# Delta-rule decoder, one core: the running inverse X summed in PSUM and copied out by ScalarE, and three vector-engine operations of step 4 in another place

## The chip, the core and the metric

The kernel runs on one core of a Trainium2 chip. A core has TensorE (PE, with its weight loads shown apart as PEld), VectorE (DVE), ScalarE (ACT), GpSimd (POOL) and SyncE (SP, which only issues transfers here). Each takes its own instructions strictly in order and waits on semaphores that others raise. The metric is device time in microseconds (us) of one execution; less is better.

## The reference

The whole is a decoder block over x (4 batches, 512 tokens, 128 features): a spiking gated delta-rule attention with a feed-forward part, then cross attention, then a three-layer feed-forward net. The change lies in the first part alone, whose recurrence is, per token, batch and head (8 heads, key size 64, value size 128):

```python
mem = DECAY * mem + sdt
hard = (mem > THR).astype(x.dtype)
spike = sur + jax.lax.stop_gradient(hard - sur)
mem = mem - spike * THR
alpha = jax.nn.sigmoid(abt + alpha_spike * spike)
beta = jax.nn.sigmoid(bbt[..., None] + jnp.sum(spike * beta_spike, axis=-1, keepdims=True))
...
s = s * alpha[..., None]
u = jnp.einsum('bhd,bhdv->bhv', kt, s)
s = s - beta[..., None] * jnp.einsum('bhd,bhv->bhdv', kt, u)
s = s + beta[..., None] * jnp.einsum('bhd,bhv->bhdv', kt, vt)
out = jnp.einsum('bhdv,bhd->bhv', s, qt)
```

The kernel doesn't run it token by token. It takes chunks of 64 tokens, so that the corrections inside a chunk become a triangular system of 64 by 64 for each head. The inverse of that system is what the change is about.

## The kernel before

**Rounds.** There are 8 chunks times 4 batches = 32 rounds, one chunk of one batch with all 8 heads in each. `rounds(body)` calls the same `body` on every engine for i = -3 to 32, and one call works on several rounds at once: `prev` (i-1) is written out, `cur` (i) reads and updates the state, `nxt` (i+1) has its triangular matrix inverted, `aft` (i+2) has the matrix entries formed level by level, and `aft2` (i+3) gets its first level. `gate` and `gate_old` (chunk gates i+7 and i+6, up to i = 24 and 25) compute alpha and beta for later chunks, and `scan` (up to i = 20) runs 32 single operations of the spike recurrence, `charge` (L199) and `fire` (L203) by turns, each of which needs the one before it. They are strewn between the other operations of the vector engine by `spike(scan, h)`.

**Steps.** A body has five steps, l = 1 to 5. In step l, TensorE runs for `nxt` `make_z` (L970: Z = E·X for this level), `make_x` (L980, for l up to 4) and `make_xt` (L994), and then for `aft` `level` (L935: the matrix entries of level l). Before, what `make_x` leaves in PSUM is added to X in SBUF by the vector engine (`add_x`, L642), what `make_xt` leaves is added to the transposed inverse XT by `add_xt` (L647), and ScalarE copies Z out of PSUM between them (`copy_z`, L1285). After `level`, the vector engine runs `prefix` (L608), `suffix` (L620) and `keep` (L637) for `aft`; `level` of step l+1 waits for the three of step l.

**What stands around them.** On TensorE in step 3: `values(cur)` (L1003) between Z and X, `correct(cur)` (L1011) and `turn_out(prev)` (L1089: transposes of the normalised output) after `level`; in step 4 `solve(cur)` (L1020), `spike_sums` and `spike_counts` of the gate; in step 5 `read_state` (L1034), `write_state` (L1082). On ScalarE: four `square` (L1330) in steps 1 and 2, `normalise(prev)` (L1338, four activations, after which `turn_out` may run) and `keep_res` (L1318) in step 3, `keep_u` (L1322), `start_xt` (L1295, L1297) and `keep_out` (L1357, whose end `read_state` of step 5 waits for) in step 4, `soft_alpha` (L1345) and `fade` (L1312) in step 5, `copy_start` (L1302: the first X of `aft`) last. On the vector engine: `scale_key` (L590) and `scale_query` (L594) of `aft2`, and `alpha` (L674) of the gate in step 5. `level` of step 5 waits for `alpha`, since both use the same PSUM banks.

All orders are written out by hand in the four `body` functions; no scheduler changes them.

Of the kernel before, what the change touches and what calls it, by code (L numbers as in the profile page):

```python
# [25 lines left out]
def decoder_kernel(nc, x, ctx_in, vec_in, wq, wk, w_spike, wv, w_out, w_au, w_ad, w_beta, w_u1, w_u2,  # L26
# [6 lines left out]
    C = 64  # L33
# [11 lines left out]
    with ctx:  # L45
# [216 lines left out]
        psZX = paired(6)  # L262
        psZX_half = psZX[:, :, 0:W]
        psXT = psG[:, B * C:B * C + HP * W].rearrange("p (a n) -> p a n", a=HP)
# [55 lines left out]

        x0_out = psZX[:, :, 0:C]

# [59 lines left out]
        def by_chunk(t):  # L382
            return t.rearrange("p (b t) -> p b t", b=B)

        GATES = NC * HP
# [16 lines left out]
        with nc.Block() as block:  # L402
# [142 lines left out]
            def _(ve):  # L545
# [50 lines left out]
                def prefix(n, l):  # L596
                    ve.wait_ge(lvl_mm, n.it * LEVELS + l + 1)
                    ve.wait_ge(kq_ok, n.it * NKQ + l + 1)
# [31 lines left out]
                def keep(n, l):  # L630
# [6 lines left out]
                    ve.copy_predicated(kept, late, level_out(l).rearrange("p a x j t -> p x a j t")).then_inc(e_ok, 1)  # L637

                def add_x(n, l):
                    ve.wait_ge(x_mm, n.it * NX + l)  # L640
                    at_ = first_half(X, l)
                    ve.tensor_tensor(at_, at_, packed(psZX_half, l), ALU.add).then_inc(x_ok, 1)  # L642

# [52 lines left out]
                def body(prev, cur, nxt, aft, aft2, gate, gate_old, scan, ramp):  # L696
                    for l in range(1, NINV + 1):
                        h = 6 * (l - 1)
                        if ramp == 0 and l != 3:
                            four_scales(1 + l // 4, (l % 4) // 2 if l < 4 else l - 4)  # L700
                        if ramp == 1 and l < 3:
                            four_scales(3, l - 1)
                        spike(scan, h)
                        if nxt and l < NINV:
                            add_x(nxt, l)
                        if l == 5 and gate:
                            alpha(gate)
# [11 lines left out]
                        spike(scan, h + 4)  # L719
                        if aft:  # L720
                            keep(aft, l)
                        spike(scan, h + 5)
# [97 lines left out]
            def _(pe):  # L820
# [88 lines left out]
                def level(n, l, gate=None, gate_old=None):  # L909
# [4 lines left out]
                    if n.it == 0 and l == 0:  # L914
# [4 lines left out]
                        pe.wait_ge(qk_ok, NQK)  # L919
                    pe.wait_ge(kq_ok, n.it * NKQ + l + 1)  # L920
                    if l == 0:
# [17 lines left out]
                def turn_start(n):  # L939
                    if n.it == 0:  # L940
                        pe.wait_ge(sd_ok, NSD)
                        pe.wait_ge(qk_ok, NQ_ALL)
                    pe.wait_ge(x_init, n.it + 1)
                    pe.wait_ge(x_ok, n.it * NX)
                    for head in by_time:
                        (rows, a), (to, q) = at_xt(*head), at_x(*head)
                        last = pe.matmul(x0_out[to, q], XT[rows, n.two, a], eye[rows], start=True, stop=True)
                    last.then_inc(x0_mm, 1)
# [11 lines left out]
                def make_z(n, l):  # L960
# [7 lines left out]
                    for head in by_time:  # L968
                        (rows, a), (_, q), (to, z) = at_level(*head), at_x(*head), at_z(*head)
                        last = pe.matmul(packed(psZX_half, l)[to, z], EA[rows, n.three, l, a], first_half(X, l)[rows, q],  # L970
                                         start=True, stop=True)
                    last.then_inc(z_mm, 1)

                def make_x(n, l):
# [227 lines left out]
            def _(ac):  # L1202
# [80 lines left out]
                def copy_z(n, l):  # L1283
                    ac.wait_ge(z_mm, n.it * NINV + l)
                    ac.copy(first_half(Z[:, l - 1], l), packed(psZX_half, l)).then_inc(z_ok, 1)  # L1285

# [13 lines left out]
                def copy_start(n):  # L1300
                    ac.wait_ge(x0_mm, n.it + 1)
                    ac.copy(X, x0_out).then_inc(x0_ok, 1)  # L1302

# [57 lines left out]
                def body(prev, cur, nxt, aft, aft2, gate, gate_old, scan, ramp):  # L1361
                    for l in range(1, NINV + 1):
# [5 lines left out]
                        if l == 1 and gate_old:  # L1368
                            soft_beta(gate_old)
                        if l == 1 and prev:  # L1370
                            square(prev, 0)
                            square(prev, 1)
                        if l == 2 and nxt:
                            keep_ks(nxt)
                        if l == 2 and prev:
                            square(prev, 2)
                            square(prev, 3)
# [4 lines left out]
                        if l == 4 and cur:  # L1382
                            keep_u(cur)
                        if l == 4 and aft:
                            start_xt(aft)
                        if l == 4 and prev:
                            keep_out(prev)
                        if l == 5 and gate:
# [906 lines left out]
```

## Time and profile before

| | |
|---|---|
| time, median of 3 runs | 1092.09 us (1091.55 to 1096.4) |
| the profiled execution | 1096.75 us, span 1095.0 us |
| share of the span busy | PE 89%, PEld 59%, DVE 64%, ACT 44%, POOL 19% |

"Busy" is the time in which an engine had at least one instruction in flight; waiting for semaphores isn't in it. The span has three parts: a prologue to about 154 us, the rounds to about 704 us, and cross attention with the last net from there. A row of the timeline gives start, length, engine, line, what is written from what, how many instructions, and in brackets how long the engine sat idle before and who ended that. The line numbers are those of the kernel before; in the changed kernel the same functions stand some 5 to 10 lines lower.

### The profile page before, as it was taken

What the parts mean: (1) busy time and instruction counts of PE and PEld (TensorE: products, weight loads), DVE (VectorE), ACT (ScalarE), POOL (GpSimd) and SP (SyncE); (2) the same over time, 40 slices, a digit from 0 to 9 for tenths busy, and PEclk for the clock granted to TensorE, in tenths of its full rate; (3) what the DMA queues carried; (4) which work ended last, traced back from release to release, by engine and by line L of the source; (5) the groups of instructions that cost most, each with busy time, mean ns of one, the idle gap of its engine ahead of it and who ended that gap; (6) DMA issues with size and microseconds to landing.
All of it is one profiled execution on the core that took longest, in us unless ns stands there. A gap on an engine that the chain in (4) does not pass through costs nothing. (4 is left out here: it accounts for less than half of the span.)

```text
span 1095.0 us, 40049 instructions
## 1 busy us (share of the span) xinstructions
PE 972.4 (89%) x16722; PEld 648.9 (59%) x16722; DVE 698.6 (64%) x2514; ACT 482.7 (44%) x1378; POOL 208.7 (19%) x394
## 2 busy tenths in 40 slices
PE   7878768999998999999999888679999999999996
PEld 2333247777777777777777777446446546546542
DVE  2887886989889888898877765145424524714710
ACT  7667412555555555545555555313323423423311
POOL 7100201122122121221221220221210310310300
PEclk8999956999999999999999999889999999999999
DMA  3000000000000000000000000211000000100100
GB/s 97 0 1 1 1 1 3 4 4 4 4 4 4 4 4 4 4 4 4 4 5 11 22 4 4 96 37 27 7 1 21 24 1 15 27 1 3 31 1 10
DMA packets 18652, 13.83 MB, mean 13 GB/s; under 512 B 2491, under 2 KB 17259, under 8 KB 18475
## 3 DMA queue, kind: packets, MB, share of 16 engines
q1 hardware_dynamic: 18475, 11.28, 3.5%
q8 instruction: 135, 2.21, 0.9%
q14 instruction: 42, 0.34, 0.1%
HBM read 7.70 MB, written 1.05 MB: 8 GB/s over the span
## 5 line engine op out<-in xcount | busy, mean ns | idle before, releaser
L935 PE MATMUL banks<-work 64*64 64x64 f32 x3072 | 97.9, 234 | 24.9 <-DVE gates L674 12.9
L994 PE MATMUL banks<-work 64*64 64x32 f32 x2560 | 107.6, 224 | 5.8 <-ACT work L1351 5.0
L1285 ACT COPY work<-banks 128x128 f32<-128x128 f32 x160 | 42.8, 268 | 157.8 <-PE banks L970 157.7
L199 DVE SCALAR_TENSOR_TENSOR gates<-mom,gates 128x16 f32<-128x16 f32 x512 | 101.1, 197 | 9.5 <-ACT gates L1258 4.5
L203 DVE SCALAR_TENSOR_TENSOR mom<-gates 128x16 f32<-128x16 f32 x512 | 102.9, 201 | 5.0
L994 PEld LDWEIGHTS banks<-work 64*64 64x64 f32 x2560 | 92.5, 139 | 18.1 <-issue 10.0
L637 DVE COPY_PREDICATED gates<-work,banks 128x256 f32<-128x256 uint32 x192 | 101.9, 531 | 1.1
L935 PEld LDWEIGHTS banks<-work 64*64 64x64 f32 x3072 | 73.0, 139 | 43.2 <-issue 20.5
L531 POOL TENSOR_TENSOR mom<-mom 128x4 f32<-128x4 f32 x32 | 7.2, 223 | 384.4 <-ACT work L1330 384.4
L608 DVE TENSOR_TENSOR work<-work 128x256 f32<-128x256 f32 x160 | 67.8, 424 | 19.3 <-PE banks L935 18.7
L647 DVE TENSOR_TENSOR work<-work,banks 128x128 f32<-128x128 f32 x160 | 45.6, 285 | 48.4 <-PE banks L994 45.4
L970 PE MATMUL banks<-work,gates 64*64 64x32 f32 x2560 | 72.7, 221 | 2.1 <-issue 1.5
L970 PEld LDWEIGHTS banks<-work,gates 64*64 64x64 f32 x2560 | 59.4, 137 | 10.2 <-issue 7.1
L980 PEld LDWEIGHTS banks<-work 64*64 64x64 f32 x2048 | 42.8, 137 | 37.1 <-issue 22.0
L1698 PE MATMUL banks<-qT,gates 128*128 128x512 f32 x128 | 59.2, 598 | 3.4 <-ACT kT L1983 2.6
L980 PE MATMUL banks<-work 64*64 64x32 f32 x2048 | 57.0, 228 | 5.8 <-ACT work L1285 2.6
L642 DVE TENSOR_TENSOR work<-work,banks 128x128 f32<-128x128 f32 x128 | 36.6, 286 | 32.3 <-PE banks L980 31.8
L1312 ACT ACTIVATE work<-work 128x128 f32<-128x128 f32 x128 | 40.9, 390 | 23.9 <-PE banks L1034 23.9
L1629 POOL TENSOR_TENSOR work<-work,half 128x4 f32<-128x4 f32 x16 | 16.1, 1009 | 185.2 <-DVE work L2099 185.2
L620 DVE TENSOR_TENSOR work<-work 128x128 f32<-128x128 f32 x160 | 46.8, 293 | 0.0
L1633 POOL TENSOR_TENSOR work<-work,gates 128x1232 f32<-128x1232 f32 x12 | 27.0, 2248 | 102.5 <-DVE gates L2205 102.5
L1034 PE MATMUL banks<-work 64*64 64x128 f32 x512 | 41.9, 278 | 5.1 <-ACT kT L1357 5.0
(263 smaller groups left out, 2140.8 us busy)
## 6 DMA issues: line engine op xcount, KB each, us to landing
work<-gates SPq DMA_DIRECT2D x28, 38.5 KB
qT<-in_x_dram SPq DMA_DIRECT2D x4, 256.0 KB, 3.8
work<-in_x_dram SPq DMA_DIRECT2D x4, 256.0 KB, 2.9
out_dram<-work SPq DMA_DIRECT2D x4, 256.0 KB, 2.3
gates<-in_w_ff_dram SPq DMA_DIRECT2D x3, 256.0 KB, 3.2
wv_sb<-in_wv_dram SPq DMA_DIRECT2D x1, 512.0 KB, 4.6
work<-in_w_out_dram SPq DMA_DIRECT2D x1, 512.0 KB, 4.0
gates<-in_x_Wq_dram SPq DMA_DIRECT2D x1, 512.0 KB, 5.0
```

The lines of the kernel that those rows point to most:

```text
L199: ve.scalar_tensor_tensor(mem[:, :, t], neg_mem, -0.9, mem[:, :, t], ALU.mult, ALU.add).then_inc(charged, 1)
L203: ve.scalar_tensor_tensor(neg_mem, mem[:, :, t], 1.0, mem[:, :, t], ALU.is_gt, ALU.subtract)\
L608: ve.tensor_tensor(second, second, by, ALU.mult).then_inc(kq_ok, 1)
L620: ve.tensor_tensor(first, first, by, ALU.mult).then_inc(ks_ok, 1)
L637: ve.copy_predicated(kept, late, level_out(l).rearrange("p a x j t -> p x a j t")).then_inc(e_ok, 1)
L647: ve.tensor_tensor(at_, at_, packed(psXT, l), ALU.add).then_inc(xt_ok, 1)
L935: last = pe.matmul(level_out(l)[to, a], KS[rows, n.two, hp], late[rows, hp], start=True, stop=True)
L970: last = pe.matmul(packed(psZX_half, l)[to, z], EA[rows, n.three, l, a], first_half(X, l)[rows, q], start=True, stop=True)
L980: last = pe.matmul(packed(psZX_half, l)[to, q], XT[rows, n.two, a], first_half(Z[:, l - 1], l)[rows, z], start=True, stop=True)
L994: last = pe.matmul(packed(psXT, l)[rows, a], Z[rows, l - 1, z], second_half(XT[:, n.two], l)[rows, a], start=True, stop=True)
L1285: ac.copy(first_half(Z[:, l - 1], l), packed(psZX_half, l)).then_inc(z_ok, 1)
L1698: last = pe.matmul(ps[:, :], w1_sb[:, a, f * P:(f + 1) * P], H1(b)[:, a, :], start=a == 0, stop=a == F2 - 1)
```

## The change

1. X lives in PSUM. Each head has 256 columns in the pair of banks; X takes the first 64, and each level's Z now has 32 columns of its own behind them. `turn_start` opens the sum and `make_x` adds to it by accumulation. `make_x` now writes the columns of X that belong to it, blocks of 2, 4, 8 and 16 columns with gaps as long, where before it wrote 32 adjacent ones.
2. `add_x` (vector engine) is gone. ScalarE has `copy_x` in its place, after `make_x` of the same step: PSUM to SBUF, half of X's columns.
3. ScalarE's order: a `square` on either side of `copy_x` in steps 1 and 2; `copy_x` ahead of `normalise` in step 3; `keep_u`, `copy_x`, `keep_out`, `start_xt` in step 4.
4. Vector engine, step 4: `scale_query` and two scan operations stand ahead of `add_xt`, and nothing of them is left behind `keep`. `prefixed` adapts the count that `prefix` and `level` wait for.

```diff
-                        if nxt and l < NINV:
-                            add_x(nxt, l)
                         if l == 5 and gate:
                             alpha(gate)
                         spike(scan, h + 1)
+                        if l == 4 and aft2:
+                            scale_query(aft2)
+                        if l == 4:
+                            spike(scan, h + 2)
+                            spike(scan, h + 3)
                         if nxt:
                             add_xt(nxt, l)
                         if l == 4 and gate:
                             drive(gate)
-                        spike(scan, h + 2)
+                        spike(scan, h + (4 if l == 4 else 2))
                         if aft:
                             prefix(aft, l)
-                        spike(scan, h + 3)
+                        spike(scan, h + (5 if l == 4 else 3))
...
-                        if l == 4 and aft2:
-                            scale_query(aft2)
...
+        def prefixed(n, l):
+            early = l == LEVELS - 1 and n.it + 1 < ROUNDS
+            return n.it * NKQ + l + 1 + early
...
-                        last = pe.matmul(packed(psZX_half, l)[to, q], XT[rows, n.two, a],
-                                         first_half(Z[:, l - 1], l)[rows, z], start=True, stop=True)
+                        last = pe.matmul(first_half(x_out, l)[to, q], XT[rows, n.two, a],
+                                         first_half(Z[:, l - 1], l)[rows, z], start=False, stop=l == NX,
+                                         skip_group_check=True)
...
+                def copy_x(n, l):
+                    ac.wait_ge(x_mm, n.it * NX + l)
+                    ac.copy(first_half(X, l), first_half(x_out, l)).then_inc(x_ok, 1)
```

ScalarE, one body in the middle of the rounds. Before (L1285 is `copy_z`):

```order
L1285 COPY work<-banks 128x64x2
L1351 ACTIVATE work<-banks,vec 128x256
L1330 ACTIVATE work,mom<-banks 128x128 x2
L1285 COPY work<-banks 128x32x4
L1306 COPY work<-banks 128x256
L1330 ACTIVATE work,mom<-banks 128x128 x2
L1285 COPY work<-banks 128x16x8
L1338 ACTIVATE work<-banks,mom 128x128 x4
L1318 COPY work<-banks 128x512
L1285 COPY work<-banks 128x8x16
L1322 COPY work<-banks 128x512
L1295 COPY work<-gates 128x128
```

The same place now, steps 3 and 4 (L1291 is `copy_z`, L1295 `copy_x`, L1348 `normalise`, L1328 `keep_res`, L1332 `keep_u`, L1367 `keep_out`, L1305 and L1307 `start_xt`):

```order
L1291 COPY work<-banks 128x16x8
L1295 COPY work<-banks 128x16x8
L1348 ACTIVATE work<-banks,mom 128x128 x4
L1328 COPY work<-banks 128x512
L1291 COPY work<-banks 128x8x16
L1332 COPY work<-banks 128x512
L1295 COPY work<-banks 128x8x16
L1367 COPY qT<-banks 128x2x2x64
L1367 COPY kT<-banks 128x2x2x64
L1305 COPY work<-gates 128x128
L1307 COPY work<-gates 64x128 x2
```

In step 3 one copy came between `copy_z` and `normalise`; in step 4 `keep_out` and `start_xt` have changed places.

Vector engine, end of step 4 and start of step 5. Before, from `suffix` (L620) to `alpha` (L674):

```order
L620 TENSOR_TENSOR work<-work 128x8x16
L199 SCALAR_TENSOR_TENSOR gates<-mom,gates 128x16
L637 COPY_PREDICATED gates<-work,banks 128x2x8x16
L203 SCALAR_TENSOR_TENSOR mom<-gates 128x16
L594 TENSOR_TENSOR work<-qT,gates 128x256
L199 SCALAR_TENSOR_TENSOR gates<-mom,gates 128x16
L674 SCALAR_TENSOR_TENSOR gates<-banks,work 128x4x64
```

The same place now (L626 is `suffix`, L643 `keep`, L675 `alpha`):

```order
L626 TENSOR_TENSOR work<-work 128x8x16
L643 COPY_PREDICATED gates<-work,banks 128x2x8x16
L199 SCALAR_TENSOR_TENSOR gates<-mom,gates 128x16
L675 SCALAR_TENSOR_TENSOR gates<-banks,work 128x4x64
```

Between `suffix` and `alpha` two scan operations and `scale_query` have gone; they stand ahead of `add_xt` of step 4. TensorE's order is the same in both kernels.

## Rows read from the trace of the kernel before

**Rows 1.** Busy time by stretch; columns as its own header says.
```profile
core 0: us, PE busy (x) PEld busy (x) DVE busy (x) ACT busy (x) POOL busy (x), PEclk, DMA share, GB/s
154.40:194.95 40.55, 36.06 (x830) 29.50 (x832) 28.62 (x132) 10.07 (x31) 5.12 (x14) 0.63 0.01 3
194.95:532.18 337.23, 310.91 (x9366) 248.91 (x9363) 293.14 (x1361) 179.76 (x640) 75.43 (x180) 1.00 0.02 4
532.18:597.36 65.18, 61.17 (x1882) 49.64 (x1880) 47.65 (x151) 35.61 (x129) 14.71 (x36) 1.00 0.02 4
```

**Rows 2.** `copy_start` (L1302), once a body: 195 to 532 us, then 532 to 597.
```profile
L1302 ACT COPY work<-banks x20: 347/372/373, 194.9 to 515.4; 128x256 f32<-128x256 f32 x20
...
L1302 ACT COPY work<-banks x4: 349/350/374, 532.2 to 581.3; 128x256 f32<-128x256 f32 x4
```

**Rows 3.** TensorE's waits, 195 to 532 us: us in total, times, longest.
```profile
PE banks L935 <- DVE gates L674: 9.9, 20, 0.6
PE banks L930 <- DVE gates L637: 4.9, 17, 0.3
PE banks L994 <- ACT work L1351: 4.0, 20, 0.2
PE banks L935 <- DVE gates L637: 3.0, 15, 0.2
```

**Rows 4.** Timeline, end of step 4 and start of step 5 of one body.
```profile
411.58 0.51 ACT L1345 ACTIVATE work<-gates,vec 128x256 f32<-128x256 f32 x1
411.73 0.18 DVE L199 SCALAR_TENSOR_TENSOR gates<-mom,gates 128x16 f32<-128x16 f32 x1
411.82 0.43 DVE L637 COPY_PREDICATED gates<-work,banks 128x256 f32<-128x256 uint32 x1
412.14 0.43 PEld L994 LDWEIGHTS banks<-work 64*64 64x64 f32 x11
412.16 0.19 DVE L203 SCALAR_TENSOR_TENSOR mom<-gates 128x16 f32<-128x16 f32 x1
412.26 0.42 DVE L594 TENSOR_TENSOR work<-qT,gates 128x256 f32<-128x256 f32 x1
412.59 0.19 DVE L199 SCALAR_TENSOR_TENSOR gates<-mom,gates 128x16 f32<-128x16 f32 x1
412.69 0.42 DVE L674 SCALAR_TENSOR_TENSOR gates<-banks,work 128x256 f32<-128x256 f32 x1
413.16 0.15 PEld L935 LDWEIGHTS banks<-work 64*64 64x64 f32 x4 [0.59 <-DVE gates L674]
```

**Rows 5.** Timeline, step 3 of the same body.
```profile
404.53 0.27 ACT L1285 COPY work<-banks 128x128 f32<-128x128 f32 x1 [1.20 <-PE banks L970]
404.78 1.14 ACT L1338 ACTIVATE work<-banks,mom 128x128 f32<-128x128 f32 x4
405.42 0.43 PE L980 MATMUL banks<-work 64*64 64x32 f32 x16
405.92 0.29 DVE L642 TENSOR_TENSOR work<-work,banks 128x128 f32<-128x128 f32 x1
406.94 0.66 PE L1089 MATMUL banks<-ident,work 128*128 128x128 f32 x4
407.09 0.58 ACT L1318 COPY work<-banks 128x512 f32<-128x512 f32 x1 [1.17 <-PE banks L1011]
407.78 0.65 PE L1020 MATMUL banks<-work 64*64 64x128 f32 x16
```

**Rows 6.** TensorE's wait for `keep_out`, 597 to 704 us.
```profile
PE banks L1034 <- ACT kT L1357: 5.0, 6, 1.3
```

**Rows 7.** Timeline, step 4 of a body without gates.
```profile
639.56 0.30 ACT L1295 COPY work<-gates 128x128 f32<-128x128 f32 x1
640.38 0.36 ACT L1357 COPY qT<-banks 128x256 f32<-128x256 f32 x1
641.16 0.55 PE L1034 MATMUL banks<-work 64*64 64x128 f32 x6 [0.44 <-ACT kT L1357]
```

**Rows 8.** Groups by shape, 195 to 530 us: busy us, mean ns, idle before.
```profile
L642 DVE TENSOR_TENSOR work<-work,banks 128x128 f32<-128x128 f32 x80 | 22.6, 282 | 9.0 <-PE banks L980 8.7
L1285 ACT COPY work<-banks 128x128 f32<-128x128 f32 x100 | 26.8, 268 | 97.2 <-PE banks L970 97.2
L980 PE MATMUL banks<-work 64*64 64x32 f32 x1280 | 34.9, 224 | 2.2
L1011 PE MATMUL banks<-work 64*64 64x128 f32 x320 | 13.6, 272 | 0.1
```

More of the change, by code:

```diff
@@ L319, in level_out, with z_out @@
             return level_at.rearrange("p a (x j t) -> p a x j t", x=2, t=1 << l)
-        x0_out = psZX[:, :, 0:C]
+        x_out = psZX[:, :, 0:C]
+        def z_out(l):
+            return psZX[:, :, C + W * (l - 1):C + W * l].rearrange("p a (j t) -> p a j t", t=1 << l)
         def counts(g):
@@ L712, in body @@
                             drive(gate)
-                        spike(scan, h + 2)
+                        spike(scan, h + (4 if l == 4 else 2))
                         if aft:
                             prefix(aft, l)
-                        spike(scan, h + 3)
+                        spike(scan, h + (5 if l == 4 else 3))
                         if aft:
                             suffix(aft, l)
-                        spike(scan, h + 4)
+                        if l != 4:
+                            spike(scan, h + 4)
                         if aft:
                             keep(aft, l)
-                        spike(scan, h + 5)
+                        if l != 4:
+                            spike(scan, h + 5)
                         if l == 1 and gate:
@@ L919, in level @@
                         pe.wait_ge(qk_ok, NQK)
-                    pe.wait_ge(kq_ok, n.it * NKQ + l + 1)
+                    pe.wait_ge(kq_ok, prefixed(n, l))
                     if l == 0:
@@ L946, in turn_start @@
                         (rows, a), (to, q) = at_xt(*head), at_x(*head)
-                        last = pe.matmul(x0_out[to, q], XT[rows, n.two, a], eye[rows], start=True, stop=True)
+                        last = pe.matmul(x_out[to, q], XT[rows, n.two, a], eye[rows], start=head[0] == 0, stop=False,
+                                         skip_group_check=True)
                     last.then_inc(x0_mm, 1)
@@ L969, in make_z @@
                         (rows, a), (_, q), (to, z) = at_level(*head), at_x(*head), at_z(*head)
-                        last = pe.matmul(packed(psZX_half, l)[to, z], EA[rows, n.three, l, a], first_half(X, l)[rows, q],
-                                         start=True, stop=True)
+                        last = pe.matmul(z_out(l)[to, z], EA[rows, n.three, l, a], first_half(X, l)[rows, q],
+                                         start=False, stop=True, skip_group_check=True)
                     last.then_inc(z_mm, 1)
@@ L1284, in copy_z @@
                     ac.wait_ge(z_mm, n.it * NINV + l)
-                    ac.copy(first_half(Z[:, l - 1], l), packed(psZX_half, l)).then_inc(z_ok, 1)
+                    ac.copy(first_half(Z[:, l - 1], l), z_out(l)).then_inc(z_ok, 1)
+                def copy_x(n, l):
+                    ac.wait_ge(x_mm, n.it * NX + l)
+                    ac.copy(first_half(X, l), first_half(x_out, l)).then_inc(x_ok, 1)
                 def start_xt(n):
@@ L1301, in copy_start @@
                     ac.wait_ge(x0_mm, n.it + 1)
-                    ac.copy(X, x0_out).then_inc(x0_ok, 1)
+                    ac.copy(X, x_out).then_inc(x0_ok, 1)
                 def keep_ks(n):
@@ L1369, in body @@
                             soft_beta(gate_old)
-                        if l == 1 and prev:
-                            square(prev, 0)
-                            square(prev, 1)
                         if l == 2 and nxt:
                             keep_ks(nxt)
-                        if l == 2 and prev:
-                            square(prev, 2)
-                            square(prev, 3)
+                        if l < 3 and prev:
+                            square(prev, 2 * l - 2)
+                        if l == 4 and cur:
+                            keep_u(cur)
+                        if nxt and l < NINV:
+                            copy_x(nxt, l)
+                        if l < 3 and prev:
+                            square(prev, 2 * l - 1)
                         if l == 3 and prev:
@@ L1381, in body @@
                             keep_res(cur)
-                        if l == 4 and cur:
-                            keep_u(cur)
+                        if l == 4 and prev:
+                            keep_out(prev)
                         if l == 4 and aft:
                             start_xt(aft)
-                        if l == 4 and prev:
-                            keep_out(prev)
                         if l == 5 and gate:
```

8 lines of the change are left out of this document (2 added, 6 removed).

## The prediction

> **What bounds the kernel now.** I read first the busy time by stretch, to see which engine fills the rounds. Over 195 to 532 us, with TensorE's granted clock at 1.00 (its 2.4 GHz level), PE is busy 310.91 of 337.23 us and the vector engine 293.14 [rows 1]. Both are near full, so the share alone doesn't say which one binds. The count of `copy_start` gives the length of a body: 20 bodies in 337.23 us are 16.86 us each, and 4 bodies in 65.18 us are 16.3 us each [rows 1, 2]. The second stretch is the test: the scan has ended there, and the vector engine does 47.65 / 4 = 11.9 us a body where it did 293.14 / 20 = 14.7 us. It lost 2.8 us of work, and the body became only 0.56 us shorter. So the vector engine's load is not what binds; TensorE's order of work is, with whatever it waits for. I then read TensorE's waits: in 20 bodies it waits 9.9 us for `alpha` (20 times), 4.9 us for the last `keep` before `level` 0, 4.0 us for `soft_beta`, 3.0 us for other `keep`s [rows 3]. Together 21.8 us, 1.1 us a body. It never waits for `add_x`. An edit gains what it takes from this list, and loses what it adds to it.
>
> **Taking `add_x` off the vector engine.** It removes 4 operations of 282 ns a body [rows 8], 1.13 us. No row of TensorE's waits names L642, and the vector engine itself waits for PE there (8.7 us in 80) [rows 8]. In step 3 of the body I followed, `add_x` ran at 405.92, right behind `make_x`, while TensorE went on with `make_xt` [rows 5]. The waits of 3.0 us on `keep` are at the ends of chains that begin at `level`, behind `add_x`. I take 0 for this edit, with 3.0 us as the most that it can give; below nothing it can't go, since it only removes work from an in-order engine.
>
> **`scale_query` and two scan operations moved.** Here the gain lies. At the end of step 4, `keep` starts at 411.82, `scale_query` at 412.26, `alpha` at 412.69, and TensorE's `level` of step 5 starts at 413.16 after 0.59 us of waiting [rows 4]. Gone from ahead of `alpha` are: the slot of `scale_query`, 412.59 - 412.26 = 0.33; of one scan operation behind `keep`, 412.26 - 412.16 = 0.10; of one ahead of it, 411.82 - 411.73 = 0.09. Sum 0.52 us, so `alpha` starts at 412.17. What else could hold it then: `soft_alpha` ends at 411.58 + 0.51 = 412.09, just earlier. TensorE's own work ahead of `level` ends at 412.14 + 0.43 = 412.57, and `alpha` would let it go at 413.16 - 0.52 = 412.64. So nearly the whole wait goes: 9.9 us less 20 times some 0.02 = **9.5 us**. The moved operations land in the time in which the vector engine waits for `make_xt` of step 4, so they cost nothing; were that cover gone, they would cost 0.52 us a body again, and the gain would be 0. Behind `level` the chain to the next wait (`level`, `prefix`, `suffix`, `keep`, `level` 0) moves as a whole, so its 4.9 us stay. Bounds: 0 to 9.9.
>
> **`copy_x` on ScalarE, steps 1, 2 and 4.** I take 0.27 us for it, the time of `copy_z`, of the same size and source [rows 8]. In these steps ScalarE is free soon enough and X is needed only by the next step's `make_z`, which TensorE reaches after `make_xt` and `level`. ScalarE's busy time would go from 180 to about 202 of 337 us, so it has the room.
>
> **`copy_x` in step 3: a new wait.** ScalarE is in order, and `copy_x` now stands ahead of `normalise` and `keep_res`. Before, `normalise` started at 404.78, right behind `copy_z`. `make_x` starts only at 405.42, since `values` stands between; its result was taken by the vector engine at 405.92. So `copy_x` can run from 405.92 to 406.19, and `normalise`, 1.14 us long, until about 407.32. TensorE's `turn_out`, which waits for it, started at 406.94 [rows 5]. With 0.05 us for the signal it now starts at 407.37: 0.43 us late. TensorE is in order, so `make_z` of step 4, `solve` and all the rest stand behind it. `keep_res`, behind `normalise` too, runs from 407.32 to 407.90, and `solve`, moved from 407.78 to 408.21, doesn't feel it. Does a later wait soak this up? The chain to `alpha` starts at `level` of step 4, behind `turn_out`, and moves along; nor do I find another. This holds for each i from 1 to 30 (both `prev` and `nxt` there): 30 times 0.43 = **12.9 us lost**. Bounds: nothing, if something in the body soaks it up, and 16 us if the strided copy takes as long as the copy of 256 columns, 0.37 us [rows 2].
>
> **ScalarE's step 4.** In the last bodies, which have no gates, TensorE waits for `keep_out`: 5.0 us in six waits, the longest 1.3 [rows 6]. `keep_out` now stands ahead of `start_xt`. In the body that I followed `start_xt` began at 639.56 and `keep_out` at 640.38 [rows 7]: 0.82 us, of which `copy_x` takes about 0.26, so it comes 0.56 us sooner. A wait of 0.44 goes whole; a wait of 1.3 keeps 0.7. With two waits below 0.56 and four above I get about 3.2 us; `start_xt`, later by 0.9 us, then presses on `copy_z` of step 5, so I take **3.0 us**. Bounds: 0 and 3.4.
>
> **The accumulating matmuls.** They take as many passes as before. No row of before shows an accumulating write with gaps; `correct` accumulates without gaps at 272 ns for 128 columns, `make_x` overwrites at 224 ns for 32 [rows 8]. As a lower end I take 0, as an upper end the length of a group with four times the columns: `solve` 0.65 against `make_x` 0.43 [rows 5], 0.22 us, four times in 30 bodies = 26 us. I take 0: `correct` and `solve`, of one size, the one accumulating and the other not, follow one another in step 3 and 4 without a difference that I could price.
>
> **The sum.** 1096.75 - 9.5 - 3.0 + 12.9 = 1097.2 us for the profiled execution. That one lies 4.7 us above the median of the runs, 1092.09; carried over, **1092.5 us**. Two true effects, each about 1%, cancel. A measurement of this kernel can tell some 0.5%, 5.5 us, from no change.
>
> **Rivals.** (A) The vector engine binds after all: it is busy 87% of the rounds, and each operation of it costs time. Then 20 bodies save 1.13 us, 22.6 us, and the time is about 1070. Against it stand the bodies without the scan. (B) The new wait in step 3 is hidden, because ScalarE gets `copy_x` done sooner or TensorE reaches `turn_out` later than in the body that I followed: 1092.1 - 12.5 = 1079.6. For it: an intermediate value would do much the same, and one body is a small sample. Against it: `make_x` to `turn_out` is 1.5 us here, and copy, `normalise` and signals need 2. (C) Slower: the wait in step 3 comes as worked out, but `alpha` doesn't come sooner, because it waits for `soft_alpha`, which ends only 0.08 us ahead of the new place [rows 4]. It decides from the point at which ScalarE reaches step 5 over 0.5 us late, by `start_xt` behind `keep_out`. Then 1092.1 + 12.9 - 3.0 = 1102. (D) The writes with gaps make `make_x` slow: up to 1092.5 + 26 = 1118.
>
> On (D) the Trainium skill speaks: the page "PSUM — Partial Sum Buffer", section Specifications, says that PSUM has cachelines of 8 bytes and that any access pattern that isn't contiguous slows matmuls significantly. "Advanced Engine Details and Errata", section PSUM Cachelines, adds that every two consecutive elements should be contiguous. By the first, all four `make_x` are hit; by the second none, since the smallest block here is two elements. No run here shows either.
>
> **How the numbers follow.** The forecast, all terms as summed: 0.52. (A) 0.07, (B) 0.15, (C) 0.18, (D) 0.08. The forecast's own range, from the bounds of its terms near the values taken, is 1087 to 1098. A range that holds the time 8 times in 10 must take in (B) and (C): 1079 to 1103, which leaves out (A) and (D), 0.15. Faster by over 0.5%: (A), (B) and 0.02 of the forecast's edge, 0.24. Slower: (C), (D), 0.26. Within: 0.50.
>
> **What the profile will show.** TensorE's waits: L935 for `alpha` falls from 9.9 us to under 1; a new row for `turn_out` waiting for `normalise`, about 0.4 us in each body; L1034's wait for `keep_out` falls from 5.0 to about 2. ScalarE waits for `make_x` in step 3. The vector engine's busy time in the rounds falls by 36 us, and it idles more. I am wrong if `turn_out` shows no wait, if `alpha` still holds `level`, or if `make_x` got longer.

## The result

Over 20 runs of each kernel the median went from 1095.3 to 1088.4 us. The ratio of the runs, after to before, is **0.9934**, with a 95% interval of 0.9913 to 0.9955: 0.66% faster, some 7 us, where I had forecast no change. The forecast stood on a base of three runs (1092.1 us), which lies 3 us below the median of these 20, so ratios and differences are compared here and not bare times. The profiled execution of after took 1094.59 us (span 1092.9) and lies high among its runs, so I compare stretches and not spans.

The same 20 bodies that took 337.23 us before [rows 1] take 330.02 us now (columns of the first line: us, then busy time by engine, granted clock):

```profile
core 0: us, PE busy (x) PEld busy (x) DVE busy (x) ACT busy (x) POOL busy (x), PEclk, DMA share, GB/s
194.84:524.86 330.02, 307.61 (x9368) 246.82 (x9366) 287.25 (x1281) 191.55 (x722) 74.66 (x180) 1.00 0.02 4
654.00:671.00 17.00, 16.04 (x464) 13.63 (x464) 7.84 (x24) 9.07 (x37) 1.21 (x2) 0.80 0.01 3
```

That is 7.2 us, the whole of the gain. The last line shows why the profiled execution isn't as fast as its rounds: near the end of the rounds TensorE, busy 16.04 of 17.00 us, was granted a mean clock of 0.80, part of the time the lower level of 1.2 GHz. In the same stretch of before it was busy 14.85 us and was granted 1.00. I draw nothing from it.

TensorE's waits over those bodies, answering to [rows 3] (us in total, times, longest):

```profile
PE banks L1000 <- ACT work L1361: 4.0, 20, 0.2
PE banks L934 <- DVE gates L643: 3.8, 13, 0.3
PE banks L939 <- DVE gates L643: 3.6, 18, 0.2
PE banks L1095 <- ACT work L1348: 1.8, 7, 0.3
PE banks L951 <- issue: 1.6, 2, 0.8
PE banks L1079 <- issue: 1.2, 3, 0.5
PE banks L1017 <- issue: 0.8, 2, 0.5
PE banks L975 <- issue: 0.7, 1, 0.7
```

The wait for `alpha`, 9.9 us before, is gone. `turn_out` (L1095) now waits for `normalise` (L1348), as forecast, but by this view for 1.8 us where I had worked out 0.43 us in each body. And rows with "issue" as the releaser have come up, 4.3 us in these four where before had 1.1: in them the view names nothing that TensorE waited for. What they are is worked out near the end.

The view of waits counts only what stands out as a gap between matmuls whose ends are modelled, so it isn't a full account. A better one is the time from the start of one group of matmuls to the start of the next, taken from the timeline and averaged over the same 20 bodies of each kernel (in before those from 196 to 533 us). Only few places move from before to after; the rest agree within 0.05 us. For use below, all kernels stand in it:

```
from -> to (us, mean)      before after  e1    e2    e3    e4    e5    e6    e7    e8
make_xt 2 -> level 2        0.78  0.83  0.84  0.81  0.83  0.83  0.82  0.83  0.63  0.63
level 2 -> make_z 3         0.45  0.28  0.48  0.27  0.30  0.28  0.27  0.45  0.31  0.30
make_xt 3 -> level 3        0.53  0.53  0.49  0.52  0.53  0.52  0.50  0.87  0.93  0.40
correct -> turn_out         0.62  0.86  0.61  0.82  0.58  1.00  0.61  0.60  0.57  0.64
make_xt 5 -> level 5        1.15  0.62  0.63  1.15  0.61  0.62  0.63  0.63  0.63  0.64
turn_start -> level 0       1.57  1.64  1.62  1.57  1.69  1.64  1.63  1.68  1.49  1.51
whole body                 16.86 16.50 16.51 16.82 16.47 16.73 16.36 16.95 16.57 16.12
```

The line of whole bodies is good to some 0.1 us: e3 and e5 differ only in the order of ScalarE's step 4, every other line agrees within 0.06 us, and the bodies still differ by 0.11.

Before to after: -0.53 at level 5 (`alpha`), +0.24 at `turn_out`, -0.17 between level 2 and `make_z` of step 3, and about +0.1 spread over several places. Sum -0.36 us a body, 7.2 us in 20.

Step 3 of one body of after, which answers to [rows 5] (L1291 is `copy_z`, L985 `make_x`, L1295 `copy_x`, L1348 `normalise`, L1095 `turn_out`, L1026 `solve`):

```profile
399.63 0.27 ACT L1291 COPY work<-banks 128x128 f32<-128x128 f32 x1 [0.87 <-PE banks L975]
400.51 0.43 PE L985 MATMUL banks<-work 64*64 64x32 f32 x16
401.02 0.27 ACT L1295 COPY work<-banks 128x128 f32<-128x128 f32 x1 [1.12 <-PE banks L985]
401.18 1.15 ACT L1348 ACTIVATE work<-banks,mom 128x128 f32<-128x128 f32 x4
402.38 0.65 PE L1095 MATMUL banks<-ident,work 128*128 128x128 f32 x4 [0.28 <-ACT work L1348]
403.22 0.65 PE L1026 MATMUL banks<-work 64*64 64x128 f32 x16
```

From the start of `make_x` to `turn_out` it is 1.87 us. `make_x`, now accumulating and writing with gaps, takes 0.43 us for its 16, exactly as before [rows 5]; the median of one matmul of it is 219 ns in both traces. And `normalise` starts 0.16 us after `copy_x` starts, not 0.27.

### The profile page after: what moved, and what is told of

It is laid out like the page before. It is cut to its first block and busy times, and to the rows that moved or that the text cites. A ratio compares the mean times of both kernels' runs of the same rounds, so it can differ in the third digit from the quotient of the medians.

```text
span 1092.9 us, 40049 instructions
## 1 busy us (share of the span) xinstructions
PE 978.3 (90%) x16722; PEld 652.6 (60%) x16722; DVE 682.3 (62%) x2386; ACT 503.7 (46%) x1506; POOL 208.7 (19%) x394
## 3 DMA queue, kind: packets, MB, share of 16 engines
q8 instruction: 135, 2.21, 0.8%
## 5 line engine op out<-in xcount | busy, mean ns | idle before, releaser
L1291 ACT COPY work<-banks 128x128 f32<-128x128 f32 x160 | 42.8, 268 | 134.1 <-PE banks L975 134.0
L199 DVE SCALAR_TENSOR_TENSOR gates<-mom,gates 128x16 f32<-128x16 f32 x512 | 98.5, 192 | 9.5 <-ACT gates L1264 4.5
L1000 PEld LDWEIGHTS banks<-work 64*64 64x64 f32 x2560 | 93.5, 140 | 18.2 <-issue 10.2
L643 DVE COPY_PREDICATED gates<-work,banks 128x256 f32<-128x256 uint32 x192 | 101.8, 530 | 1.1
L648 DVE TENSOR_TENSOR work<-work,banks 128x128 f32<-128x128 f32 x160 | 45.8, 286 | 88.5 <-PE banks L1000 86.6
L939 PEld LDWEIGHTS banks<-work 64*64 64x64 f32 x3072 | 74.3, 140 | 31.4 <-issue 20.7
L985 PEld LDWEIGHTS banks<-work 64*64 64x64 f32 x2048 | 43.7, 139 | 38.1 <-issue 22.6
L985 PE MATMUL banks<-work 64*64 64x32 f32 x2048 | 57.8, 230 | 6.0 <-ACT work L1291 2.7
L1295 ACT COPY work<-banks 128x128 f32<-128x128 f32 x128 | 34.5, 269 | 43.1 <-PE banks L985 42.8
L626 DVE TENSOR_TENSOR work<-work 128x128 f32<-128x128 f32 x160 | 46.3, 289 | 0.0
```

The lines of the kernel that those rows point to most:

```text
L199: ve.scalar_tensor_tensor(mem[:, :, t], neg_mem, -0.9, mem[:, :, t], ALU.mult, ALU.add).then_inc(charged, 1)
L626: ve.tensor_tensor(first, first, by, ALU.mult).then_inc(ks_ok, 1)
L648: ve.tensor_tensor(at_, at_, packed(psXT, l), ALU.add).then_inc(xt_ok, 1)
L939: last = pe.matmul(level_out(l)[to, a], KS[rows, n.two, hp], late[rows, hp], start=True, stop=True)
L985: last = pe.matmul(first_half(x_out, l)[to, q], XT[rows, n.two, a], first_half(Z[:, l - 1], l)[rows, z], start=False, stop=l == NX, skip_g ...
L1000: last = pe.matmul(packed(psXT, l)[rows, a], Z[rows, l - 1, z], second_half(XT[:, n.two], l)[rows, a], start=True, stop=True)
```

## The experiments

Each was timed against the kernel before on the same chip: e1 to e4 on one, e5 to e7 on another, e8 on a third.

### e1: the vector engine's moves alone

The kernel before with `scale_query` and two scan operations ahead of `add_xt` in step 4; X stays in SBUF.

```diff
+                        if l == 4 and aft2:
+                            scale_query(aft2)
+                        if l == 4:
+                            spike(scan, h + 2)
+                            spike(scan, h + 3)
                         if nxt:
                             add_xt(nxt, l)
...
-                        if l == 4 and aft2:
-                            scale_query(aft2)
```

> The kernel before with the vector engine's moves of step 4 alone (scale_query and two scan operations ahead of add_xt); X stays in SBUF, add_x stays on the vector engine. Theory of waits (W): the wait of level 5 for alpha, 9.9 us in 20 bodies, goes whole, nothing else moves: ratio to before 0.991, about -10 us; the row of L935 waiting for alpha falls under 1 us. Rival (V), the gain of the changed kernel comes from the vector engine's lighter load: this one has the same load, so 1.000.

Measured: 0.9939 (0.9918 to 0.996). The vector engine has the same work as before (busy 296.3 us in the 20 bodies, before 293.1) and nearly the whole gain is there, so the lighter load isn't its cause. TensorE's wait for `alpha` is gone from the list. The gain is 6.7 us and not 10, which lies just outside what the interval allows (4.4 to 9.0 us). Some came back as issue rows:

```profile
PE banks L1082 <- issue: 1.4, 3, 0.8
PE banks L956 <- issue: 0.8, 1, 0.8
PE banks L944 <- issue: 0.7, 2, 0.4
PE banks L979 <- issue: 0.7, 2, 0.4
```

### e2: X in PSUM alone

The changed kernel with the vector engine's step 4 in its old order.

```diff
-                        if l == 4 and aft2:
-                            scale_query(aft2)
-                        if l == 4:
-                            spike(scan, h + 2)
-                            spike(scan, h + 3)
                         if nxt:
                             add_xt(nxt, l)
...
+                        if l == 4 and aft2:
+                            scale_query(aft2)
```

> The changed kernel with the vector engine's step 4 in its old order: X in PSUM, copy_x and ScalarE's new order stay. W: the wait for alpha is back (about 10 us); turn_out waits for normalise, about +0.24 us in each of 30 bodies (+7 us); make_z of step 3 no longer waits for add_x of step 2 (-0.17 us a body, -3 to -5 us); keep_out comes sooner in the last bodies (-3 us). Sum -1 to +1 us, ratio 0.999 to 1.001. V: most of the gain stays, 0.994.

Measured: 1.0015 (0.9993 to 1.0037), which agrees with the 0.999 to 1.001 expected. This half of the change takes four operations a body from the vector engine (busy 283.5 us in the 20 bodies, before 293.1) and gains nothing: the wait for `alpha` is back, and `turn_out` waits.

```profile
PE banks L934 <- DVE gates L675: 9.8, 20, 0.5
PE banks L929 <- DVE gates L643: 5.5, 19, 0.3
PE banks L1090 <- ACT work L1343: 2.2, 8, 0.3
```

It also isolates the term that I had missed. With `copy_x` on ScalarE, `make_z` of step 3 starts 0.27 us after level 2 (column e2 of the table); in both kernels with `add_x`, before and e1, it is 0.45 and 0.48. The rows of before show why, once one looks at the right place (L642 is `add_x`, L970 `make_z`):

```profile
403.56 0.35 PEld L935 LDWEIGHTS banks<-work 64*64 64x64 f32 x16 [0.28 <-issue]
403.62 0.28 DVE L642 TENSOR_TENSOR work<-work,banks 128x128 f32<-128x128 f32 x1
404.01 0.35 PEld L970 LDWEIGHTS banks<-work,gates 64*64 64x64 f32 x16
```

Here the weight loads of level 2 end at 403.91, `add_x` ends at 403.90, and `make_z` begins at 404.01. `add_x` of step 2 stands behind `keep` of step 1, which is also what level 2 waits for, so both come out together, and the next `make_z` needs `add_x`. The start of that `make_z` lies 0.15 us behind the end of `add_x` in all 20 bodies of before, in 19 of 20 of e1 and in 19 of 20 of e6, so it is `add_x` that lets it go, and 0.45 us is not TensorE's own pace. In after, `copy_x` was done long before:

```profile
398.22 0.27 ACT L1295 COPY work<-banks 128x128 f32<-128x128 f32 x1
398.79 0.42 PEld L939 LDWEIGHTS banks<-work 64*64 64x64 f32 x16 [0.29 <-issue]
399.10 0.35 PEld L975 LDWEIGHTS banks<-work,gates 64*64 64x64 f32 x16
```

### e3: `copy_x` of step 3 behind `normalise`

```diff
-                        if nxt and l < NINV:
+                        if nxt and l < NINV and l != 3:
                             copy_x(nxt, l)
...
                         if l == 3 and prev:
                             normalise(prev)
+                        if l == 3 and nxt:
+                            copy_x(nxt, l)
```

> The changed kernel with copy_x of step 3 behind normalise instead of ahead of it. W: turn_out doesn't wait any more; that gives back 0.24 us in each of 30 bodies, about 7 us: ratio to before 0.987. By the step of my prediction (0.43 us a body, 12.9 us) it would be 0.982. If the wait is hidden anyway: 0.993 as the changed kernel.

Measured: 0.9901 (0.9873 to 0.9928). In the trace the wait of `turn_out` is gone (0.86 to 0.58 in the table). The time is 0.0033 better than that of the change, under half of what 0.28 us a body would give, and the two intervals overlap. The bodies became only 0.03 us shorter in this profile; waits with issue as releaser took the difference:

```profile
PE banks L1079 <- issue: 2.0, 3, 0.7
PE banks L951 <- issue: 1.8, 2, 1.1
PE banks L939 <- issue: 1.7, 5, 0.6
PE banks L975 <- issue: 1.0, 2, 0.6
```

### e4: a second copy ahead of `normalise`

```diff
                     ac.wait_ge(x_mm, n.it * NX + l)
-                    ac.copy(first_half(X, l), first_half(x_out, l)).then_inc(x_ok, 1)
+                    if l == 3:
+                        ac.copy(X[:, 0:2], x_out[:, 0:2])
+                        ac.copy(X[:, 2:4], x_out[:, 2:4]).then_inc(x_ok, 1)
+                    else:
+                        ac.copy(first_half(X, l), first_half(x_out, l)).then_inc(x_ok, 1)
```

> The changed kernel with copy_x of step 3 done as two copies of 128x128 (whole X of two heads of four each), so that normalise starts one ScalarE slot, about 0.17 us, later. W: the time from the start of make_x to turn_out has a floor, 1.86 us in the changed kernel; it becomes 2.03, and only bodies that were above it already hide the rest: 24 of 30 bodies lose up to 0.17 us, about +4 us over the changed kernel, ratio to before 0.997. If the wait is soaked up elsewhere: 0.993.

Measured: 0.9956 (0.9938 to 0.9974), 0.0022 slower than the change, in the direction and about half of the size expected; the two intervals overlap. In the table `turn_out` comes 0.15 us later (0.86 to 1.00), close to the slot of 0.17. And the time from the start of `make_x` to `turn_out`, whose floor was expected to go from 1.86 to 2.03 us, is 2.03 or 2.04 in 17 of the 20 bodies. So the delay follows the length of what stands ahead of `normalise`. In time this shows best between e4 and e3, which differ only in what stands there: 0.9956 and 0.9901, 0.0055 apart with intervals that don't meet, some 6 us where the table's 0.43 us in 30 bodies makes 13.

```profile
PE banks L1095 <- ACT work L1352: 6.4, 18, 0.5
```

### e5: `start_xt` ahead of `keep_out` again

```diff
+                        if l == 4 and aft:
+                            start_xt(aft)
                         if l == 4 and prev:
                             keep_out(prev)
-                        if l == 4 and aft:
-                            start_xt(aft)
```

> e3_copy_behind with ScalarE's step 4 in its old order, start_xt ahead of keep_out, copy_x where it is in the change. If the term for keep_out (3.0 us, six waits of the last bodies) was right, this is 3 us slower than e3_copy_behind: ratio to before 0.993 against 0.990. If those waits only moved elsewhere: 0.990. In the trace L1040 waits for keep_out again, near 5 us in six waits.

Measured: 0.99 (0.9867 to 0.9932), the same as e3. The waits are back in the trace:

```profile
PE banks L1040 <- ACT kT L1367: 5.2, 6, 1.3
```

From `make_z` of step 5 to `read_state` the last four bodies that have both sum to 4.86 us in before, 1.95 in after, 2.55 in e3 and 5.14 here, so the new order takes 2.6 to 2.9 us off these waits. But the time doesn't show it. Both intervals are some 3 us wide to either side, so a term of 3 us can neither be confirmed nor ruled out here. It stays open.

### e6: `add_x` of step 2 sooner

e1 with the gate's `spikes` operation behind `add_x`.

```diff
                         if nxt and l < NINV:
                             add_x(nxt, l)
+                        if l == 2 and gate:
+                            spikes(gate)
...
-                        if l == 1 and gate:
-                            spikes(gate)
```

> e1_move_only (X in SBUF, add_x on the vector engine) with the gate's spikes operation, 0.29 us, moved from the end of step 1 to behind add_x of step 2. Theory: make_z of step 3 starts 0.45 us after level of step 2 where 0.25 is its pace, because it waits for add_x of step 2; this edit starts add_x 0.2 us sooner, so that start comes at 0.27 or less, about 0.17 us a body in 20 bodies, 3.4 us: ratio to before 0.991 against 0.994 of e1_move_only. Rival, that the 0.45 us are TensorE's own pace: 0.994 and an unchanged 0.45.

Measured: 0.9976 (0.9953 to 0.9998), slower than e1. A miss. `add_x` of step 2 started with level 2 as before (0.01 us behind its start, 0.03 in e1) and the 0.45 us stayed, so the edit didn't test what it was meant to test: two scan operations that need one another now stand side by side, the second starts 0.26 us after the first where 0.1 is usual.

```profile
268.20 0.22 DVE L203 SCALAR_TENSOR_TENSOR mom<-gates 128x16 f32<-128x16 f32 x1
268.46 0.19 DVE L199 SCALAR_TENSOR_TENSOR gates<-mom,gates 128x16 f32<-128x16 f32 x1
268.56 0.28 DVE L646 TENSOR_TENSOR work<-work,banks 128x128 f32<-128x128 f32 x1
```

What it lost is a new wait: level 3 (L944) waited 5.9 us in 14 for `beta` (L685), the last operation of step 2.

### e7: the scan out of the chains

e3, with no scan operations between `prefix`, `suffix` and `keep` in steps 1 and 5. They stand behind `keep`, in step 1 two of them behind `spikes`; the last two of step 5 stand between the updates of the state that follow it.

```diff
-                        spike(scan, h + (5 if l == 4 else 3))
+                        tight = l == 1 or l == 5
+                        if not tight:
+                            spike(scan, h + (5 if l == 4 else 3))
                         if aft:
                             suffix(aft, l)
-                        if l != 4:
+                        if l != 4 and not tight:
                             spike(scan, h + 4)
                         if aft:
                             keep(aft, l)
                         if l != 4:
-                            spike(scan, h + 5)
+                            spike(scan, h + (3 if tight else 5))
                         if l == 1 and gate:
                             spikes(gate)
+                        if l == 1:
+                            spike(scan, h + 4)
+                            spike(scan, h + 5)
...
```

> e3_copy_behind with the scan operations taken out from between prefix, suffix and keep in steps 1 and 5 and put behind keep. TensorE waits there for keep: L934 about 4.3 us in 15 waits and L939 3.6 us in 18. Each chain gets two slots of 0.1 us shorter, so about 0.2 us a wait: -3 to -7 us against e3_copy_behind, ratio to before 0.984 to 0.987. Rival: what TensorE saves in waits it now waits for its own instructions (rows with issue as the releaser, 1.1 us before, 6 us or more in the faster kernels): ratio 0.989 to 0.990, and the issue rows grow by as much as the keep rows fall.

Measured: 0.9911 (0.9883 to 0.9938), no better than e3. Neither theory held as written. The two chains got shorter by 0.2 us each (rows 1 and 6 of the table), but level 3 lost 0.40, waiting for `beta`. The rows for `keep` fell from 7.9 us in e3 to nothing and the issue rows grew only from 6.9 to 8.4 (from 195 to 532 us, all rows):

```profile
PE banks L948 <- DVE gates L682: 6.8, 13, 0.7
PE banks L1009 <- ACT work L1370: 4.2, 21, 0.2
PE banks L948 <- issue: 2.8, 6, 0.9
```

### e8: the scan's operations where the vector engine waits

e7 with one scan operation fewer in step 1, two fewer in step 2, one fewer at the end of step 5, and eight instead of four ahead of `add_xt` of step 4 (the expectation below counts them wrongly; the edit is this one). A counter (`step`) takes the place of `spike(scan, h + ...)`.

```diff
-                        spike(scan, h)
+                        step()
                         if l == 5 and gate:
                             alpha(gate)
-                        spike(scan, h + 1)
+                        step()
                         if l == 4 and aft2:
                             scale_query(aft2)
                         if l == 4:
-                            spike(scan, h + 2)
-                            spike(scan, h + 3)
+                            step(6)
                         if nxt:
                             add_xt(nxt, l)
...
+                        if 1 < l < 5:
+                            step()
                         if aft:
                             suffix(aft, l)
...
+                        if l == 3:
+                            step()
                         if aft:
                             keep(aft, l)
...
```

> e7_short_chains with five scan operations fewer in steps 1, 2 and 5 and six more ahead of add_xt of step 4, where the vector engine waits over 1 us for TensorE; beta of step 2 so comes sooner. e7 lost at level 3, which waited for beta (6.8 us in 13 waits), what it had won at levels 2 and 0. If beta came late because of the scan operations ahead of it, that wait falls under 2 us and the kernel gains 4 to 6 us over e7 and 3 to 5 us over e3_copy_behind: ratio to before 0.985 to 0.987. Rival: TensorE waits for its own instructions instead (rows with issue as releaser grow), ratio 0.990.

Measured: **0.9808** (0.978 to 0.9836), median 1077.95 us: better than both kernels, and by more than I expected. The waits for `beta`, `keep` and `alpha` are all but gone; what is left is `soft_beta` and the issue rows, of which these are the largest:

```profile
PE banks L1012 <- ACT work L1373: 4.2, 21, 0.2
PE banks L951 <- issue: 2.4, 4, 0.9
PE banks L963 <- issue: 1.8, 2, 1.3
PE banks L987 <- issue: 1.5, 4, 0.6
PE banks L951 <- DVE gates L675: 0.2, 1, 0.2
```

The vector engine is busy 290.86 us in the 20 bodies here, more than the 287.25 of the changed kernel, and yet the bodies are 0.38 us shorter. Against e3, whose other edits e8 shares, the table has -0.20 us at level 2, -0.18 at level 0 and -0.13 at level 3.

```profile
196.13:518.50 322.37, 306.20 (x9364) 246.52 (x9362) 290.86 (x1282) 192.31 (x722) 74.68 (x180) 1.00 0.02 4
```

## Why the prediction was wrong

**The bound was right.** That the vector engine's load doesn't bind, and its place in TensorE's waits does, is what e1 and e2 show: all of the gain without a lighter load, and no gain with one. Rival (A) is out. How much lighter the load gets was misjudged: I had forecast 36 us less busy time in 32 bodies, which is 22.6 in 20, and it fell by 5.9 (293.14 to 287.25), and by 9.7 in e2. An operation's length isn't the busy time that it adds, since it overlaps its neighbours.

**`alpha` was right.** Expected 0.52 us a body; level 5 comes 0.53 us sooner, in after and in e1. `soft_alpha` didn't hold it, so rival (C) is out.

**The step that failed is "`copy_x` in step 3: a new wait".** The mechanism was right, and its size was not: 0.43 us a body, 12.9 us, where the table has 0.24 us, 7.2 us if all 30 bodies are like the 20. With 12.9 the losses cancelled the gains of 12.5, and so the forecast was no change. Two errors have the same sign.

First, I let `normalise` begin when `copy_x` ended. On ScalarE the next operation begins before the one ahead of it has ended: `copy_x` starts at 401.02 and `normalise` at 401.18, a slot of 0.16 and not 0.27 us. The trace of before had it in `normalise` itself, whose four activations of 368 ns take 1.14 us together [rows 5], so 0.26 us from one to the next:

```profile
L1338 ACT ACTIVATE work<-banks,mom 128x128 f32<-128x128 f32 x80 | 22.8, 368 | 1.9 <-POOL mom L533 1.9
```

I had used slots for the vector engine and a length for ScalarE. With the signal that makes a floor of 1.86 us from `make_x` to `turn_out`, where I had 1.95.

Second, I took one body for all. It had 1.52 us from `make_x` to `turn_out`, the least that occurs. Over the 20 bodies of before the mean is 1.69, with single ones up to 2.30; in after it is 1.86 in nearly all, mean 1.92. A new floor costs a body only what that body is below it: 0.34 us for the one I had followed, and 0.20 us on average if the floor of 1.86 is laid under the 20 distances of before. Measured are 0.23 to 0.24; in three bodies of after something else held `turn_out` (2.10 to 2.44). I had named this under rival (B), as half of it hidden, and given it no time between 0 and 12.9.

**A term was missing.** I wrote that TensorE never waits for `add_x`, and put its removal at 0, from a view in which it isn't listed. It cost 0.17 us a body in step 2, 3.4 us in 20 bodies, hidden in that view because the matmuls of level 2 run, by their modelled ends, until 404.06, and `make_z` starts at 404.04: there is no gap to list. Comparing the distance between two groups in different steps (0.45 us in step 2, 0.29 and 0.28 in steps 1 and 4) would have shown it.

**`make_x` with gaps** costs nothing: 0.43 us for 16 as before. Rival (D) is out. Of what I had cited from the Trainium skill, the sentence of "PSUM Cachelines" in "Advanced Engine Details and Errata", that every two consecutive elements should be contiguous, agrees with the trace. The sentence in "PSUM — Partial Sum Buffer", section Specifications, that any non-contiguous pattern slows matmuls significantly, doesn't hold for these blocks of 2 to 16; "PSUM Cachelines" has that sentence too, which I hadn't said.

**`keep_out`** did what was said in the trace (5.0 us to 1.3), and its worth in time is open (e5).

**The sum again**, for the 20 bodies: -10.6 (`alpha`) + 4.8 (`turn_out`) - 3.4 (`add_x`) + 2.0 (issue and small things) = -7.2 us. For the whole kernel, with a wait of 0.24 and the missing 3.4 us, the forecast's own sum would have been -9.5 - 3.0 + 7.2 - 3.4 = -8.7 us. Measured is a change of -6.9 us, with an interval of -9.5 to -4.9. So the two mended terms suffice to bring the forecast into the interval. That the forecast's bare 1092.5 us lies only 4 us from the 1088.4 measured is luck: its base was 3 us low. One thing pulls the other way and was in no term, the issue rows.

**What the issue rows are: TensorE waits for instructions.** In before there were two of them in the 20 bodies:

```profile
PE banks L970 <- issue: 0.6, 3, 0.2
PE banks L957 <- issue: 0.5, 2, 0.3
```

The traces tell what they are, if one counts TensorE's instructions (matmuls, weight loads and semaphore instructions, in order of start) up to each such wait of a matmul, between 154 and 700 us (rows of weight loads bear the word issue as well, and aren't counted here):

- Of the 246 waits with issue as the releaser in the ten kernels, 236 stand at a count that leaves 192 to 194 when divided by 256. The other ten are one and the same place, once in each kernel. TensorE's 845 waits with another releaser are spread over all remainders.
- In each kernel the trace has 34622 instructions of TensorE and 135 packets of 16384 bytes in the instruction queue q8, one for 256 instructions. In 1185 of the 1196 places where TensorE passed from one 256 to the next, between 154 and 700 us, as many packets had landed as it had passed such places, and no further one had started; the next one started 1.3 us later (median) and took 0.9 to 1.5 us.
- Each of the 236 waits ended 1.19 to 1.71 us after such a packet had landed. Where TensorE passed such a place without this wait, the packet had landed 1.69 to 1.94 us before (medians of the ten kernels), and in only 2 of 960 cases less than 1.19 us.

So in these 236 waits TensorE had used up the instructions that it had, and went on 1.2 to 1.7 us after the next 256 came. It needs 4.4 us for 256 instructions here (median), and the supply takes some 3.6 to 4.1 us by the numbers above (1.3 until the packet starts, 1.1 for it at the median, 1.2 to 1.7 behind it), so that an edit that shortens another wait can run into this one:

```
154 to 700 us        before after  e1    e2    e3    e4    e5    e6    e7    e8
waits with issue       16    20    20    18    29    24    28    26    34    31
us                     5.3   9.4   8.8   7.3  14.5  11.0  11.2  12.8  15.6  15.0
```

After has 4.1 us more of it than before, and e1 3.5 more, which is what its gain of 6.7 us lacks to the 10 expected. e3 has 5.1 more than after, about as much as it fell short of the 8.4 us that its 0.28 us a body would give; e4 has 3.5 less than e3. e6 has 12.8 too, and isn't fast, so these waits aren't all that a kernel's time follows. The places are fixed by the program's order and the waits come at the same ones in kernel after kernel. No run has fewer instructions for the same work, so what taking these waits away would be worth is not measured.

The Trainium skill, page "Advanced Engine Details and Errata", section ISA Cache, says that an instruction cache has lines of 16 KB, 256 instructions each. This case's trace agrees: 135 packets of instructions hold 2.21 MB, and the waits stand 256 instructions apart or a multiple of it.

## What to carry to other kernels

Before pricing a new wait, take the distance between the two instructions over all bodies and not in one: a floor costs only the bodies below it. Use the distance from start to start for every engine, not the length of an operation. TensorE's rows with issue as the releaser are to be counted in steps of 256 instructions before an edit is priced: near its pace of supply, a gain elsewhere comes back there in part. A wait that the list of waits doesn't show can be found by comparing the same pair of groups in steps that should be alike. And where an engine isn't the bound, don't take work off it but move its work: e8 has the same operations on the vector engine as e3, keeps it busy for longer (290.9 us against 286.9) and is the fastest, with eight of its scan operations, where e3 has four, ahead of `add_xt` of step 4, where that engine waits anyway. e7 and e8 together moved scan operations in steps 1, 2, 4 and 5; which move brings how much has no run of its own.

## What was not expected of the hardware

In nearly each body a scan operation of 128x16, about 0.19 us long, takes 0.35 to 0.7 us. It is one that runs beside GpSimd's multiplication for `keys` (L506) or the one behind it (L516), and it ends 0.04 to 0.05 us after that multiplication has ended. In before:

```profile
405.92 0.29 DVE L642 TENSOR_TENSOR work<-work,banks 128x128 f32<-128x128 f32 x1
406.13 0.57 DVE L203 SCALAR_TENSOR_TENSOR mom<-gates 128x16 f32<-128x16 f32 x1
406.62 0.27 DVE L647 TENSOR_TENSOR work<-work,banks 128x128 f32<-128x128 f32 x1
```
```profile
405.93 0.72 POOL L506 TENSOR_TENSOR work<-kT,gates 128x256 f32<-128x256 f32 x1 [1.19 <-DVE work L620]
406.62 0.40 POOL L516 TENSOR_TENSOR work<-gates 128x128 f32<-128x128 f32 x1
```

Here the scan operation ends at 406.70 and `keys` at 406.65. There are 20 scan operations over 0.35 us in the 20 bodies of before (8.1 us above their normal length), 21 in after (5.1), 20 in e3 (4.8), 33 in e6 (12.3), 24 in e7 (9.2) and 6 in e8 (1.5). Over all ten traces they are 204, and each ends 0.04 to 0.05 us after an operation of one of these two lines. "GPSIMD Engine Reference", Specifications, in the Trainium skill, says that GpSimd shares SBUF interfaces with the vector engine and contends with its instructions that have two inputs in SBUF; the scan operation is one. `prefix` and `suffix` have two inputs in SBUF as well, and those that overlap these two lines in before kept their length (0.42 and 0.28 us on average), so two inputs alone don't make an operation slow here. In e6 and e7 a long one stands between level 2 and `beta`, for which level 3 waits, in 15 of 20 bodies; it does so in e1 too, with less time in it, and in none of e8. It may be part of what e6 and e7 lost. How much, no run here separates.
